# Turns on GpSimd, a deviation in PSUM and a later variance in a convolution and rotation kernel

## The reference, cut to what matters

```python
# x: (16, 128, 64, 64) float32; 32 groups of 4 channels
def _gn(v, G=32, eps=1e-05):             # normalise each image's group
    g = v.reshape(B_, G, C_ // G, H_, W_)
    m = mean(g, (2, 3, 4)); s = var(g, (2, 3, 4))
    return ((g - m) / sqrt(s + eps)).reshape(v.shape)

x = x + depthwise_5x5(_gn(x), kernel_of(L0_conv_weight))
x = x + einsum('hvc,bchw->bvhw', L1_conv_rota_matrix, _gn(x))
```

## Time and profile before

| | us |
|---|---|
| median of three runs | 506.56 |
| lowest and highest | 503.28, 509.76 |
| the profiled execution | 507.81 |
| its span | 505.9 |
| TensorE busy in the span | 425.8 (84%) |
| VectorE, GpSimd, ScalarE busy | 375.6, 311.2, 300.2 |

### The profile page before, as it was taken

The page is one execution under the profiler, slowest core; times in us unless marked ns, Lnnn a source line. Parts: engine busy times, 40 slices in busy tenths (PEclk is TensorE's granted clock), DMA queues, the critical chain, the costliest instruction groups (busy, mean ns, idle before and its releaser), DMA issues.

```text
span 505.9 us, 8856 instructions
## 1 busy us (share of the span) xinstructions
PE 425.8 (84%) x3168; PEld 215.6 (43%) x3168; DVE 375.6 (74%) x654; ACT 300.2 (59%) x566; POOL 311.2 (62%) x410
## 2 busy tenths in 40 slices
PE   0097968999999999999999969944999979879890
PEld 0044424555555555555555535522444334324330
DVE  3329899999999999999999957583677455345561
ACT  1345543777767677776767737734577746464540
POOL 3496684998989899898989947213344423232320
PEclk9999998999999999999999999995899989898896
DMA  9979997999999999999999998996999999999998
GB/s 135 179 172 225 218 213 117 256 231 253 220 236 226 242 239 234 243 220 249 226 231 292 234 259 241 336 338 125 352 345 422 414 410 416 416 419 415 415 409 302
DMA packets 180443, 140.70 MB, mean 278 GB/s; under 512 B 139760, under 2 KB 141872, under 8 KB 176304
## 3 DMA queue, kind: packets, MB, share of 16 engines
q1 hardware_dynamic: 159264, 106.86, 75.5%
q10 hardware_dynamic: 20656, 33.16, 23.4%
q0 software_dynamic: 480, 0.11, 0.2%
HBM read 72.96 MB, written 67.15 MB: 277 GB/s over the span
## 4 chain that ended last, share of the span: by engine, by line
PE 59%; DMA 19%; DVE 13%; SPq 2%; issue 2%; POOL 1%; ACT 1%; ACTq 1%; POOLq 0%; DVEq 0%
PE ps L582 45%; DMA out_dram<-area 15%; PE ps L642 12%; DVE stats L497 3%; DVE dev L536 3%; DVE stats L504 2%; SPq L197 2%; DMA tap_rows<-line 2%; DVE area L560 1%; DVE area L489 1%; DMA area<-tap_rows 1%; DMA area<-in_x_dram 1%; ACTq L220 1%; ACT area L408 1%; DMA norm<-affine 1%
## 5 line engine op out<-in xcount | busy, mean ns | idle before, releaser
L582 PE MATMUL ps<-area 64*64 64x512 f32 x2560 | 292.7, 606 | 3.9 <-POOL area L338 3.8
L582 PEld LDWEIGHTS ps<-area 64*64 64x64 f32 x2560 | 146.5, 134 | 104.2 <-issue 99.7
L408 ACT ACTIVATE area<-ps 64x512 f32<-64x512 f32 x254 | 150.0, 591 | 55.7 <-PE ps L582 51.0
L338 POOL TENSOR_TENSOR area<-mask,area 128x325 f32<-128x325 f32 x128 | 153.2, 1230 | 29.0 <-PE ps L582 23.4
L642 PE MATMUL ps<-area 128*128 128x512 f32 x256 | 124.3, 637 | 19.0 <-DVE area L560 14.8
L560 DVE TENSOR_TENSOR area<-ps,area 128x512 f32<-128x512 f32 x128 | 82.0, 686 | 61.7 <-DMA out_dram<-area 43.1
L353 POOL TENSOR_SCALAR area<-area,affine 128x256 f32<-128x256 f32 x155 | 95.5, 629 | 28.9 <-DVE affine L519 24.7
L449 ACT ACTIVATE area<-area,norm 128x256 f32<-128x256 f32 x157 | 80.5, 588 | 55.0 <-PE ps L642 53.6
L382 POOL TENSOR_SCALAR area<-area,norm 128x256 f32<-128x256 f32 x95 | 52.0, 561 | 90.9 <-PE ps L642 87.9
L497 DVE BATCH_NORM_STATS2 stats<-area 128x6 f32<-128x512 f32 x128 | 80.4, 690 | 17.9 <-DMA area<-in_x_dram 17.9
L642 PEld LDWEIGHTS ps<-area 128*128 128x128 f32 x256 | 50.1, 203 | 82.6 <-issue 46.7
(11 more groups left out here) (28 smaller groups left out, 67.0 us busy)
## 6 DMA issues: line engine op xcount, KB each, us to landing
area<-in_x_dram SPq DMA_DIRECT2D x252, 128.0 KB, 4.3
x_scratch<-area ACTq DMA_DIRECT2D x62, 512.0 KB, 6.3
out_dram<-area SPq DMA_DIRECT2D x15, 2048.0 KB, 17.7
area<-x_scratch SPq DMA_DIRECT2D x25, 1024.0 KB, 14.8
area<-x_scratch SPq DMA_DIRECT2D x7, 896.0 KB, 13.4
out_dram<-area SPq DMA_DIRECT2D x2, 1024.0 KB, 10.3
area<-tap_rows SPq DMA_DIRECT2D x8, 142.2 KB
x_scratch<-area SPq DMA_DIRECT2D x2, 512.0 KB, 5.3
```

The lines of the kernel that those rows point to most:

```text
L338: last = nc.gpsimd.tensor_tensor(taps[k % TRING][:, c * KW:(c + 1) * KW].rearrange("p d (b r) -> p d b r", r=TAPS), bass.AP(tensor=of_rows ...
L408: last = nc.scalar.activation(y[k % YRING][rows, 2 * pair + c], ps[half, bank + n].rearrange("p (j w) -> p j w", j=J), ACT.Identity)
L582: last = nc.tensor.matmul(ps[half, bank + n], taps[k % TRING][rows, (2 * pair + c) * KW + d, 0:H], padded[k % GRING][rows, 2 * pair + c, : ...
```

## The change

Three things change.

On GpSimd, from step 4 on, bands and images alternate: band 0 of group s + 2, images 0 and 1 of group s + 1, band 1, images 2 and 3, band 2, image 4, band 3. The waits for taps and for the affine are functions of their own (`await_taps`, `await_norms`) and stand before the first of each. In steps below 4 the order is as it was.

On VectorE, in the rounds of steps below 4 (rounds 0 to 5), the deviation is computed twice, to SBUF and to PSUM (`dev_ps`); the square multiplies the one by the other and goes to PSUM (`dev2_ps`), and the spread reads it there.

On TensorE the places are a function of the step: 3 in steps 0 to 3, 2 in step 4, 1 in step 5, 0 from step 6 on. The means had 3 up to step 3 and 0 after it; the variance had 0 everywhere, and keeps it in step 0 and before.

```diff
+        dev2_ps = ps[:, 6, 4 * J:6 * J].rearrange("p (k j) -> p k j", k=2)
+        dev_ps = ps[:, 6, 2 * J:4 * J].rearrange("p (k j) -> p k j", k=2)
...
-            def spread_taps(k):
+            def await_taps(k):
                 if k < FIRST:
                     pool.wait_ge(taps_landed[0], 16 * TAPS)
                     pool.wait_ge(taps_landed[1], 16 * TAPS)
...
                 if k >= TRING:
                     pool.wait_ge(convolved, 2 * (k - TRING + 1))
+
+            def spread_taps(k, cs):
...
-                for c in range(GC):
+                for c in cs:
...
-            def normalise(k):
+            def await_norms(k):
                 pool.wait_ge(affine_ready, k + 1)
                 if k >= GRING:
                     pool.wait_ge(convolved, 2 * (k - GRING + 1))
-                for j in range(POOL_J):
+
+            def normalise(k, js):
+                for j in js:
...
             for s in STEPS:
-                if group(s + 1) and 0 <= s < FILL:
-                    normalise(s + 1)
-                if group(s + 2):
-                    spread_taps(s + 2)
-                if group(s + 1) and s >= FILL:
-                    normalise(s + 1)
+                if s < FILL:
+                    if group(s + 1) and s >= 0:
+                        await_norms(s + 1)
+                        normalise(s + 1, range(POOL_J))
+                    if group(s + 2):
+                        await_taps(s + 2)
+                        spread_taps(s + 2, range(GC))
+                else:
+                    if group(s + 2):
+                        await_taps(s + 2)
+                        spread_taps(s + 2, (0,))
+                    if group(s + 1):
+                        await_norms(s + 1)
+                    for c, js in ((1, (0, 1)), (2, (2, 3)), (3, (4,))):
+                        if group(s + 1):
+                            normalise(s + 1, js)
+                        if group(s + 2):
+                            spread_taps(s + 2, (c,))
...
-                    dve.wait_ge(dev_ready, r + 1)
-                    nc.vector.tensor_tensor(dev2[:, k], dev[:, k], dev[:, k], ALU.mult).then_inc(dev2_ready, 1)
+                    other, dev2 = dev, dev2_sb
+                    if s < FILL:
+                        nc.vector.tensor_tensor(dev_ps[:, k], stats[:, r % 2, k, :, 1], ps_mean[:, k],
+                                                ALU.subtract).then_inc(dev_ready, 1)
+                        other, dev2 = dev_ps, dev2_ps
+                    dve.wait_ge(dev_ready, r + 1 + min(r + 1, FILL + 2))
+                    nc.vector.tensor_tensor(dev2[:, k], dev[:, k], other[:, k], ALU.mult).then_inc(dev2_ready, 1)
...
+            def place(s):
+                return min(KW - 2, max(0, FILL + KW - 3 - s)) if s >= 0 else 0
+
             for s in STEPS:
-                first = KW - 2 if 0 <= s < FILL else 0
+                first, first_spread = place(s), place(s) if s >= 1 else 0
...
-                    if is_round(s + 1) and d < 2:
-                        average_spread(s + 1, high if d else low)
+                    if is_round(s + 1) and d in (first_spread, first_spread + 1):
+                        average_spread(s + 1, low if d == first_spread else high)
```

More of the change, by code:

```diff
@@ L115, in conv_rotate_kernel @@
         dev = sb("dev", [P, 2, J])
-        dev2 = sb("dev2", [P, 2, J])
+        dev2_sb = sb("dev2", [P, 2, J])
         spread = sb("spread", [P, 2, J])
@@ L355, in normalise @@
                                                    ALU.mult, ALU.add)
-                last.then_inc(normed_pool, 1)
+                if j == POOL_J - 1:
+                    last.then_inc(normed_pool, 1)
             def send_norms(k):
```

## The result

The changed kernel takes 525.82 us (median of 4 runs, 523.26 to 527.32), the one before 505.8 in the same session (503.28 to 509.76): **1.0397 times as long, 95% interval 1.0347 to 1.0446**. I had forecast the direction, and 516.3 us with a range up to 522; it is 20 us, not 10.

The account below looks back on a forecast made before the run. TensorE was taken to bound steady steps, DMA second. Affine 4 + 5.9 + 0.95 = 86.35, plus 24 x 9.65, gave 318.0 against 308.25 at step 29: +9.7 us, so 516.3 us against the median; range 501 to 522.

Parts of the forecast that it names:

- affine 4 at 79.5: Early steps on VectorE: the add waits for the bands instead of the square; affine 4 comes 4.1 us earlier.
- The load stall of step 28: VectorE's wait for the last load vanishes, because a 9.65 us step asks less of the DMA queues.
- rival 1: Early steps: the add is let in between two bands; no change, 505 to 509 us; chance 0.18.
- rival 2: Steady steps: turns cost TensorE nothing, the last load decides, 4.8 us earlier, 501.8 us; chance 0.10.
- rival 3: Steady steps: VectorE is not let in until GpSimd runs dry; 40 us slower; chance 0.05.
- I take the middle, 9.65.: Steady step, affine to affine: 9.6 (image first), 9.65 (square held past the band) or 9.84 us (add first).
- Fifth image of step 4 at 79.5 + 5.9: GpSimd's fifth image ends 5.9 us after affine 4; TensorE may then start step 5.
- I price it at nothing: TensorE, steps 1 to 3: variance matmuls at places 3 and 4 come 2.7 us later, at no cost.
- From step 29 on and in the rotation I change nothing.: End of the kernel: no time added or saved after the first variance row of step 29.
- worst case of the race: Add ahead of fifth image: 9.84 us a step, step 5 begun 1.1 us later; +15 us, 521.
- The ceiling: DMA queues: the last load can come at most 4.8 us earlier, limiting any gain to under 1%.
- The rule against the forecast: Shared port: a VectorE instruction asking during a train of bands waits for the train; the skill says one band.

Follow-up runs that it names:

- the turns alone: Kernel before with only GpSimd's alternating bands and images from step 4; square stays in SBUF, matmul places stay: 524.72 us, ratio 1.0377.
- the kernel without turns: Changed kernel with GpSimd's order of before (bands, then images); PSUM squares and later matmul places stay: 505.19 us, ratio 0.9986.
- the places of before: Changed kernel with variance and mean matmuls where they stood in the kernel before: 521.3 us, ratio 1.0294.
- the bands held: Kernel before; in steps 1 to 3 GpSimd begins its bands only after VectorE's first add of the step: 500.68 us, ratio 0.9911.
- the loads moved: Kernel before with the bands held, and the rotation matrices' four loads in steps 27 to 30 instead of 24 to 27: 495.79 us, ratio 0.9826.
- the kernel with one band between: Changed kernel with images 2, 3 and 4 together, so only one band lies between affine and last image: 516.63 us, ratio 1.0215.

## Why the prediction was wrong

**Right in its direction and its main mechanism.** The add took the square's wait in the early steps, up to affine 4 at 79.5 (79.55). The turns put two bands and the add ahead of the fifth image. The load stall of step 28 vanished. That the turns cause the loss is shown by the turns alone (18.5 us) and by the kernel without turns (no difference). Rivals 1, 2 and 3 of the prediction did not happen in the changed kernel's profile, though the kernel without turns shows that rival 1 can, in a single step.

**Wrong in four terms of the sum.** Counted in the profiled executions at the first variance row of step 29, which is 325.81 in the changed kernel, forecast 318.0, before 308.25:

- *"I take the middle, 9.65."* Of three outcomes the last came, add first, in every step: 9.785 us instead of 9.65, over 23 steps (6 to 28) 3.1 us. The prediction gave 9.84 as its most. It treated the order of add and fifth image as open and took a value between. In the three traces with two bands before the fifth image and the square in SBUF (the changed kernel, the turns alone, the places of before) the add went first 77 times of 77.
- *Fifth image of step 4 at 79.5 + 5.9.* The same outcome one step earlier: step 5 starts at 86.60 instead of 85.4, 1.2 us later.
- *"The variance matmuls ... I price it at nothing", and the mean matmuls of step 4 "cost nothing".* For the variance only steps 1 to 3 were looked at. Step 5 with its variance at place 1, at the low clock, took 13.2 us, 3.6 more than a steady step of the forecast. The kernel with the old places has 9.81 there.
- *"From step 29 on and in the rotation I change nothing."* Behind that row the rest of the execution took 525.0 - 325.81 = 199.2 against 505.9 - 308.25 = 197.6 us, 1.6 more. Of these, 0.9 are step 29, which still has the turns: 9.79 us between its variance row and the next, 8.88 before. Where the other 0.7 went I did not test.

The first three make 7.9 us; the variance row came 0.88 us behind the start instead of 0.95, which leaves the 7.8 of the stretch. The prediction's own worst case of the race (9.84 us a step and a later step 5) gave about 15 us and 521; the profiled executions differ by 19. So the race alone would have stayed in the range. What broke it is step 5, priced at nothing, with the 1.6 us at the end. Of the step's loss the place is 0.9 us; the rest is the clock, and why it stayed low so long is open.

The square of 6.99 us, which the prediction puts in step 4, stands in step 3, ahead of affine 4; nothing in the sum follows from that.

**The ceiling.** That gains are limited by the last load was right in kind (5.77 us idle with the bands held, none with the loads moved) and wrong in size: the gap of 4.8 us in one stretch of the DMA share was no measure of how much earlier the last load could land, which was 9.8 us with the bands held.

**The rule against the forecast.** The Trainium skill (SBUF — State Buffer, Who interferes with whom) says that whoever issues first has the shared pair for its whole instruction. By that rule a waiting request should come in after one band; mine was that a train is held. I counted in all eleven traces. Of VectorE's requests made 0.05 to 0.8 us into a band that another band follows, squares in SBUF were let in at that band's end 0 times of 9, first adds 1 of 21, second adds (behind the affine) 8 of 8. First adds that asked up to 0.03 us ahead of a band, with an image directly before it and another band behind it, were let in at that band's end 28 times of 28. Two more asked as closely ahead of a band that came out of an idle stretch, and went first. Neither rule covers all of that. What decides is open.

## What to carry to other kernels

In these traces who waits at the port was set by who follows whom. Take the wait from one instruction and look at the next one on its engine with the same operands: here it inherited the wait. Interleaving work that is needed now with work that is not delays the last needed piece. An idle piece of the other engine may be what lets a long instruction through; keep it, or make it on purpose with a wait. Where two requests meet within some hundredths of a microsecond, put the worse order into the range in full: in the changed kernel it came back in every step from 4 to 29. And when a change meets a stretch where an engine halts, look at each step of that stretch; a steady-state price does not cover it.

## What was not expected of the hardware

With halts of 4.01 and 2.82 us within 11 us, TensorE's granted clock stayed at 0.50 for 13.6 us and two places of matmuls took 3.44 us. With halts of 4.02 and 1.06 us, in the trace of the kernel with one band between, it was back at 1.00 before the step, and two places took 1.76. The places of the matmuls are the same in both; each is one trace. In the steady steps halts of 0.65 us did not lower the granted clock (1.00 from 120 to 240 us).

A VectorE instruction that waits for a GpSimd band is let in before the band's recorded end: the add of 2.12 us at 144.60 must have started at 145.50 if it ran for its usual 1.22 us, 0.14 before the band ended at 145.64. In the changed kernel the spread, let in this way, and the add behind it came ahead of the fifth image in every step.
